# Batched softmax and memory denominators in the second attention, with PSUM evacuations given to ScalarE

## The reference

```python
def step(carry, seg):
    M, z = carry
    qs, ks_, vs = seg
    sq = jax.nn.elu(qs) + 1.0
    sk = jax.nn.elu(ks_) + 1.0
    num_q = einsum('bhld,bhde->bhle', sq, M)
    den_q = einsum('bhld,bhd->bhl', sq, z)[..., None] + EPS
    a_mem = num_q / den_q
    num_k = einsum('bhld,bhde->bhle', sk, M)
    den_k = einsum('bhld,bhd->bhl', sk, z)[..., None] + EPS
    v_delta = vs - num_k / den_k
    M_new = M + einsum('bhld,bhle->bhde', sk, v_delta)
    z_new = z + sk.sum(axis=2)
    scores = einsum('bhld,bhmd->bhlm', qs, ks_) * inv_sqrt_dk
    scores = where(causal_mask, scores, finfo.min)
    a_dot = einsum('bhlm,bhme->bhle', softmax(scores), vs)
    a = gate * a_mem + (1.0 - gate) * a_dot
    return ((M_new, z_new), a)
```

## Time and profile before

| What | Value |
|---|---|
| median of 2 timed runs | 10,834.65 us (10,738.39 and 10,930.91) |
| profiled execution, its own time | 10,657.9 us |
| span in that execution, slowest core | 10,656.3 us (all cores 10,609.8 to 10,656.3) |
| busy on the slowest core | TensorE 5,201.5 us (49%), VectorE 3,776.5 (35%), ScalarE 2,896.8 (27%) |
| weight loads of TensorE | 2,420.8 us, beside its matmuls |
| mean granted TensorE clock | 0.70 of 2.4 GHz |

### The profile page before, as it was taken

How to read it: one execution, slowest core, us unless ns; L and a number is a source line. 1 busy time by engine, 2 the same in 40 slices (tenths; PEclk the granted TensorE clock), 3 DMA queues, 4 the chain that set the end, 5 groups by cost and what they waited for, 6 DMA issues and landing times.

```text
span 10656.3 us, 90473 instructions; the slowest of 8 cores (10609.8 to 10656.3 us)
## 1 busy us (share of the span) xinstructions
PE 5201.5 (49%) x25664; PEld 2420.8 (23%) x25664; DVE 3776.5 (35%) x11485; ACT 2896.8 (27%) x5090; POOL 8.6 (0%) x13
## 2 busy tenths in 40 slices
PE   3856333325585633332558563333254856333326
PEld 1322111112232311111223221111122322111113
DVE  1123344453112334445311233444531123344443
ACT  4222222222322222222132232222213223222221
POOL 0000000000000000000000000000000000000000
PEclk9877555557797855555779775555577977555558
DMA  2001000000101100001010110000101001000010
GB/s 67 12 32 38 10 1 1 16 32 32 63 16 32 34 14 1 1 16 32 32 63 16 32 36 12 1 1 16 32 33 62 16 32 40 9 1 1 16 32 32
DMA packets 69509, 257.50 MB, mean 24 GB/s; under 512 B 7584, under 2 KB 7584, under 8 KB 69024
## 3 DMA queue, kind: packets, MB, share of 16 engines
q1 hardware_dynamic: 50592, 184.60, 5.2%
q10 hardware_dynamic: 18432, 67.12, 2.0%
HBM read 218.14 MB, written 33.55 MB: 24 GB/s over the span
## 4 chain that ended last, share of the span: by engine, by line
PE 39%; DVE 26%; ACT 12%; issue 12%; DMA 9%; DVEq 2%; ACTq 0%; SPq 0%
PE pb L169 35%; PE pb L182 4%; DVE a L682 3%; ACT xn_tm L414 2%; DMA x_tm<-x 2%; ACT ebuf L889 2%; DVE xn_tm L1027 2%; DVE a L981 2%; DVEq L1158 2%; DVE ptbuf L937 2%; ACT warena L303 2%; DVE xn_tm L1049 1%; DVE a L910 1%; DVE a L675 1%; ACT ebuf L897 1%
## 5 line engine op out<-in xcount | busy, mean ns | idle before, releaser
L169 PE MATMUL pb<-a,warena 128*128 128x512 bf16 x6144 | 1446.3, 397 | 343.6 <-DVE a L682 156.8
L169 PE MATMUL pb<-xn_fm,warena 128*128 128x512 bf16 x5120 | 1170.7, 393 | 77.8 <-ACT xn_fm L448 51.3
L169 PE MATMUL pb<-xn_tm,ptbuf 128*128 128x512 bf16 (+1 forms) x3328 | 693.3, 351 | 611.8 <-DVE ptbuf L937 542.0
L169 PEld LDWEIGHTS pb<-a,warena 128*128 128x128 bf16 x6144 | 614.7, 102 | 1153.7 <-issue 540.8
L349 ACT ACTIVATE junkb<-x_tm 128x1024 bf16<-128x1024 f32 x256 | 270.4, 1056 | 2007.3 <-DVE x_tm L580 679.5
L182 PE MATMUL pb<-identb,xn_tm 128*128 128x128 bf16 x2304 | 243.9, 282 | 1084.8 <-ACT xn_tm L414 848.7
L169 PE MATMUL pb<-ebuf,warena 128*128 128x512 bf16 x2048 | 530.5, 425 | 416.6 <-DVE a L746 389.8
L1036 PE MATMUL pb<-xn_tm 128*128 128x128 bf16 x512 | 135.3, 264 | 1133.4 <-DVE xn_tm L1027 1133.4
L169 PEld LDWEIGHTS pb<-xn_fm,warena 128*128 128x128 bf16 x5120 | 510.9, 100 | 724.8 <-issue 192.0
L182 PE MATMUL pb<-identb,ebuf 128*128 128x128 bf16 x2304 | 288.1, 262 | 690.0 <-DVE ebuf L903 690.0
L169 PEld LDWEIGHTS pb<-xn_tm,ptbuf 128*128 128x128 bf16 x3328 | 299.5, 106 | 967.8 <-issue 776.1
(11 more groups left out here) (102 smaller groups left out, 6055.9 us busy)
## 6 DMA issues: line engine op xcount, KB each, us to landing
out<-x_tm SPq DMA_DIRECT2D x64, 512.0 KB, 2.7
warena<-wkfT ACTq DMA_DIRECT2D x48, 512.0 KB, 3.3
warena<-wrT SPq DMA_DIRECT2D x48, 512.0 KB, 3.4
warena<-wvfT SPq DMA_DIRECT2D x48, 512.0 KB, 3.3
x_tm<-x SPq DMA_DIRECT2D x48, 512.0 KB, 3.3
warena<-wqaT SPq DMA_DIRECT2D x24, 512.0 KB, 4.4
warena<-wkaT ACTq DMA_DIRECT2D x24, 512.0 KB, 3.3
warena<-wqb SPq DMA_DIRECT2D x24, 512.0 KB, 4.4
```

Of the source, the lines that this page charges most:

```text
L169: return e.matmul(out, lhsT, rhs, start=st, stop=sp)
```

## The change

The computation stays the same; five things differ, all in `emit_attn_b` (a column `bepscol` that holds epsilon is set up at the start):

1. In `passA` the copy of the transposed blocks to `ptbuf` is made by ScalarE instead of VectorE.
2. The row sums of the four blocks go to separate columns of `dsc`. One addition, one reciprocal and one scaling of 128x4 per head follow after the fourth block, where each block had its own three. A 128x1 memset of the first column is new.
3. The A·V products of the four blocks go side by side into bank 4. After the fourth block ScalarE evacuates them with four scaled activations of 128x128.
4. In `passB` eight matmuls with one column each give the denominators of all four blocks, for Q and K, in bank 5. ScalarE evacuates them with epsilon as bias, VectorE makes one reciprocal of 128x8 and one gate product of 128x4. The numerator matmuls have 128 columns instead of 132. The six small operations per block are gone. The value delta has the opposite sign, and the memory update subtracts it.
5. The gated memory answer is added into `adbuf` in place, and one addition of 128x4x128 per head puts it into `x_tm`, where each block had its own.

```diff
 passA(h), per block lc:
-                        pte = evac(2, "vector", lambda e, lc=lc: e.tensor_copy(
+                        pte = evac(2, "scalar", lambda e, lc=lc: e.copy(
                                        ptbuf[:, 0:lc + 1, :],
                                        pbb[2][:, 0:128 * (lc + 1)]),
                                    waits=[ptm] + buf_war.get("ptbuf", []))
-                        adm = mm_group(ab_, mms, waits=[pte, vt_last])
-                        ads = evac(ab_, "vector", lambda e, ab_=ab_, lc=lc: e.tensor_scalar(
-                                       out=adbuf[:, 128 * lc:128 * lc + 128],
-                                       in0=pb[ab_].ap()[:, 0:128],
-                                       scalar1=dsc[:, 4:5], scalar2=None, op0=ALU.mult),
-                                   waits=[adm, sdm] + buf_war.get(("ad", h % 2, lc), []))
+                        for j in range(lc + 1):
+                            def fad(e, j=j, lc=lc, h=h, st=st, sp=sp):
+                                return e.matmul(
+                                    pb[4].ap()[:, 128 * lc:128 * lc + 128],
+                                    ptbuf[:, j, :],
+                                    xn_tm[:, 4 + j, 128 * h:128 * h + 128],
+                                    start=st, stop=sp)
 passA(h), after the four blocks:
+                    zsum = dv(lambda e: e.tensor_tensor(
+                        out=dsc[:, 36:40], in0=dsc[:, 36:40],
+                        in1=dsc[:, 40:44], op=ALU.add), waits=[z2m, e1, z0m])
+                    rzb = dv(lambda e: e.reciprocal(dsc[:, 40:44], dsc[:, 36:40]), waits=[zsum])
+                    sdb = dv(lambda e, omgcol=omgcol: e.tensor_scalar(
+                        out=dsc[:, 44:48], in0=dsc[:, 40:44],
+                        scalar1=omgcol, scalar2=None, op0=ALU.mult), waits=[rzb])
+                    for lc in range(4):
+                        ads = evac(4, "scalar", lambda e, lc=lc: e.activation(
+                                       out=adbuf[:, 128 * lc:128 * lc + 128],
+                                       in_=pb[4].ap()[:, 128 * lc:128 * lc + 128],
+                                       func=AF.Identity, scale=dsc[:, 44 + lc:45 + lc]),
+                                   waits=[adm_l[3], sdb])
 passB(h), ahead of the four blocks:
+                    denm = mm_group(5, [(sqkv[:, u, h, 128 * lc:128 * lc + 128],
+                                         Maug[:, h, 128:129],
+                                         pb[5].ap()[:, 2 * lc + u:2 * lc + u + 1])
+                                        for lc in range(4) for u in range(2)],
+                                    waits=maug_ready + [el_m[1]])
+                    dev = evac(5, "scalar", lambda e: e.activation(
+                        out=dsc[:, 16:24], in_=pb[5].ap()[:, 0:8],
+                        func=AF.Identity, bias=bepscol[:, 0:1]), waits=[denm])
+                    rbm = dv(lambda e: e.reciprocal(dsc[:, 24:32], dsc[:, 16:24]), waits=[dev])
+                    gqb = dv(lambda e, gcol=gcol: e.tensor_scalar(
+                        out=dsc[:, 32:36], in0=rcp[:, :, 0:1],
+                        scalar1=gcol, scalar2=None, op0=ALU.mult), waits=[rbm])
 passB(h), per block lc:
-                               Maug[:, h, :], pb[3].ap()[:, 0:132]),
+                               Maug[:, h, 0:128], pb[3].ap()[:, 0:128]),
...
-                        d1 = dv(lambda e: e.tensor_scalar(
-                            out=dsc[:, 5:6], in0=pb[3].ap()[:, 128:129],
-                            scalar1=B_EPS, scalar2=None, op0=ALU.add), waits=[nm])
...
                         vdm = dv(lambda e, h=h, lc=lc: e.scalar_tensor_tensor(
-                            out=vd_b, in0=pb[3].ap()[:, 132:260],
-                            scalar=dsc[:, 10:11],
+                            out=vd_b, in0=pb[3].ap()[:, 128:256],
+                            scalar=rcp[:, lc, 1:2],
                             in1=xn_tm[:, 4 + lc, 128 * h:128 * h + 128],
-                            op0=ALU.mult, op1=ALU.add),
-                            waits=[rkn] + buf_war.get("vd", []))
+                            op0=ALU.mult, op1=ALU.subtract),
+                            waits=[nm, gqb] + buf_war.get("vd", []))
+                        c1_last = dv(lambda e, h=h, lc=lc: e.scalar_tensor_tensor(
+                            out=adbuf[:, 128 * lc:128 * lc + 128],
+                            in0=pb[3].ap()[:, 0:128],
+                            scalar=dsc[:, 32 + lc:33 + lc],
+                            in1=adbuf[:, 128 * lc:128 * lc + 128],
+                            op0=ALU.mult, op1=ALU.add), waits=[vdm])
 passB(h), after the four blocks:
+                    c2 = dv(lambda e, G=G, h=h, adbuf=adbuf: e.tensor_tensor(
+                        out=x_tm[:, 4 * G:4 * G + 4, 128 * h:128 * h + 128],
+                        in0=adbuf.rearrange("p (l c) -> p l c", l=4),
+                        in1=x_tm[:, 4 * G:4 * G + 4, 128 * h:128 * h + 128],
+                        op=ALU.add), waits=[c1_last])
```

More of the change, by code:

```diff
@@ L874, in passA @@
                     adbuf = adbuf_a if h % 2 == 0 else adbuf_b
+                    z0m = dv(lambda e: e.memset(dsc[:, 36:37], 0.0),
+                             waits=buf_war.get("zb1", []),
+                             tag=f"{tag}z0_{G}_{h}")
+                    e1 = z2m = None
+                    adm_l, pte_l = [], []
                     for lc in range(4):
@@ L941, in passA @@
                                    tag=f"{tag}pte{G}_{h}_{lc}")
+                        pte_l.append(pte)
                         buf_war[("E", par)] = [ptm]
[L943 to L949 removed]
@@ new lines, in passA @@
+                        adm_l.append(adm)
+                        buf_war["ptbuf"] = [adm]
+                    zsum = dv(lambda e: e.tensor_tensor(
+                        out=dsc[:, 36:40], in0=dsc[:, 36:40],
+                        in1=dsc[:, 40:44], op=ALU.add),
+                        waits=[z2m, e1, z0m], tag=f"{tag}zs_{G}_{h}")
+                    rzb = dv(lambda e: e.reciprocal(dsc[:, 40:44],
+                                                    dsc[:, 36:40]),
+                             waits=[zsum], tag=f"{tag}rz_{G}_{h}")
@@ new lines, in passA @@
+                    buf_war["zb1"] = [rzb]
+                    sdb = dv(lambda e, omgcol=omgcol: e.tensor_scalar(
+                        out=dsc[:, 44:48], in0=dsc[:, 40:44],
+                        scalar1=omgcol, scalar2=None, op0=ALU.mult),
+                        waits=[rzb] + buf_war.get("zb_sd", []),
+                        tag=f"{tag}sd_{G}_{h}")
+                    ads = None
+                    for lc in range(4):
+                        ads = evac(4, "scalar",
+                                   lambda e, lc=lc: e.activation(
+                                       out=adbuf[:, 128 * lc:128 * lc + 128],
+                                       in_=pb[4].ap()[:, 128 * lc:128 * lc + 128],
+                                       func=AF.Identity,
+                                       scale=dsc[:, 44 + lc:45 + lc]),
+                                   waits=[adm_l[3], sdb] +
+                                         buf_war.get(("ad", h % 2, lc), []),
```

123 lines of the change are left out of this document (46 added, 77 removed).

## The result

| | before | after |
|---|---|---|
| median of the timed runs | 10,746.56 us (10 runs, 10,620.18 to 10,930.91) | 10,199.43 us (11 runs, 10,123.16 to 10,399.37) |
| profiled execution, its own time | 10,657.9 us | 10,240.26 us |
| fastest execution | 10,620.18 us | 10,123.16 us |

The ratio after to before is **0.9487, 95% interval 0.9434 to 0.9540**: faster by 5.1%. The forecast ratio was 0.963. In some executions one or both groups of four cores had a lower granted clock, which adds up to 4% whatever the kernel, so the ratios with an interval leave these out, and elsewhere I read single heads or the fastest execution.

What follows compares the result with a forecast made beforehand. A latency chain with handovers, not one full engine, bounds the kernel. Terms of -399, -2, -82, +40 and +50 sum to -393 us: 10,657.9 becomes 10,265, or 10,435 on the median; range 10,250 to 10,600, widened to 10,220 to 10,670.

Steps and rivals of the forecast that it cites:

- A: passA: copy on ScalarE and softmax sums normalised once per head, from mask to A·V; gain 1.12 us per middle head.
- B: Four scaled evacuations stand ahead of the elu operations in ScalarE's queue; loss 2.96 us per middle head.
- C: Entry into passB, from its transposes to the first wide operation, with grouped denominators; gain 0.91 us per head.
- D: passB's loop of four blocks: six small operations go, spacing 3.03 to 1.45 us; gain 4.74 us per head.
- E: One 512-wide addition replaces four narrow ones and delays the next mask; loss 0.25 us per middle head.
- first passA of a segment: passA's gain there is eaten by the evacuations ahead of the next exponential; -0.1 us, 16 times.
- last passB of a segment: No passA before it and its elu ran ahead anyway; -5.15 us, 16 times, -82 in all.
- segment's end: Four row statistics wait for the one addition; loss 3.2 us in 12 segments, 0.4 in 4 before the FFN, +40.
- weight conversions: In a sequence's last segment, conversions on ScalarE lose their cover beside passB; loss 12.6 us, 4 times, +50.
- denominators: Rival: passB's one-column matmuls are not pipelined, 0.37 us each; 10,709 us; chance 0.09, shared with larger ScalarE waits.
- the clock: Rival: TensorE gets its full clock in the head loop, some 2 us less a head; 10,175 us; chance 0.05.
- function table loads: Rival: ScalarE reloads its function table between copies and exponentials, ten loads a head; 12,100 us, slower; chance 0.02.

Runs made afterwards that it cites:

- x9: The kernel before with one column per block for the first partial row sum, so most L889 wait for TensorE alone; a head 31.57 us instead of 31.70.
- x1: The changed kernel with passA as it was before, passB as changed; a head 25.91 us, fastest execution 0.940 of before.
- x2: The kernel before with the new passA only, passB as before; a head 32.77 us, fastest execution 1.011 of before.
- x10: The changed kernel with VectorE's sum over the keys moved behind the first block of passB's loop; a head 26.63 us, fastest execution 0.950 of before.

## Why the prediction was right in its direction and short in size

| term | forecast | measured | times | difference, us |
|---|---|---|---|---|
| A, passA's copies and sums | -1.12 | -1.78 | 112 | -74 |
| B, evacuations ahead of elu | +2.96 | +2.94 | 112 | -2 |
| C, entry into passB | -0.91 | -1.08 | 112 | -19 |
| D, loop of four | -4.74 | -4.84 | 112 | -11 |
| E, addition and next mask | +0.25 | +0.04 | 112 | -24 |
| first passA of a segment | -0.1 | -0.8 | 16 | -11 |
| last passB of a segment | -5.15 | -5.6 | 16 | -7 |
| segment's end | +3.2 | +5.5 | 12 | +28 |
| weight conversions | +12.6 | +10.2 | 4 | -10 |

A is measured from the first mask to the last A·V group, B from there to passB's transposes, the conversions as what a sequence's last segment takes beyond the others (12.9 us, before 2.7).

Summed with the measured terms the third layer becomes some 525 us shorter (4,744 to 4,220, core 1 before and core 4 after), the rest of the program 19 longer. The whole of these cores goes from 10,609.8 to 10,104.3, -505, a ratio of 0.952; the forecast was -393.

**The step that failed is A**, -74 of the -130 us by which the terms missed, in two sentences of it. "Score, exponentials and mask between stay" was wrong: from A·V to the next mask the three stretches shrank by 0.19 in all, of which the second wait explains most (x9: 0.12). The diff showed the wait going: "[waits sPE,sDV]" became "[waits sPE]". I had read that row and priced nothing. And "Back to TensorE I put 0.20" was too much: it is 0.14, as for VectorE (1299.54 + 0.27 to 1299.95). With copies and handovers slightly shorter than in my sum, mask to A·V sums to 5.83 instead of 6.17. The last 0.12 lies in the base: the means of before are 7.41, where I read 7.29 from one head without its stalls.

**B and D** held in mechanism and size, which x1 and x2 confirm by splitting them. Four evacuations took 1.14 from the first start to the last end. What the sum needs is the time to the next operation's start, and that was 1.02 (1283.74 to 1284.76), forecast 1.12; the three handovers took back 0.07 of it. By the figures of the page "ScalarE: Activation LUTs" of the Trainium skill, section "What ACT_TABLE_LOAD costs", that step was an estimated 1.2. The trace has 0.36 to 0.38 for one evacuation where they give 0.386, and 1.02 for the step. The spacing in D is 1.43 in the mean, where 1.45 was forecast.

**C** came out near for the wrong reason. I priced a one-column matmul like a transpose, 0.105. The group of eight takes 0.40, and one of them 0.17 in the mean:

```profile
L170 PE MATMUL pb<-a 128*128 128x1 bf16 x1024 | 50.7, 171 | 0.0
```

So they start some 0.03 apart, (0.40 - 0.17) / 7, which is below my lower bound of 0.05; in the single records the first gap is 0.07 and the other six are 0.027. The twelfth matmul ended 0.78 after the first transpose began, not 1.43, and the evacuation was done 0.48 before the reciprocal started. "VectorE is past its copy and its sum over the keys by then" failed: that sum (L1010) set the end (x10). The page "TensorE: Matmul & The Clock Gate" of the Trainium skill, section "Wait — 56ns, not 53.3ns?", puts the floor at 25 ns, and the trace agrees within 2 ns. The 0.64 that I worked out from this rule was there on TensorE (1.43 to 0.78), and the wait for the sum hid it.

**E**: I let the mask wait for the whole addition and memset. It starts 0.07 before the addition ends, and the memset runs beside it. In the first passA of a segment I had let the evacuations eat A's gain; most of it stayed (0.8).

**The segment's end** has the right mechanism, "now all four wait for the one addition", and too low a price: the statistics follow each other at 1.24, not at 1.06, since each is followed by a read of its accumulator (0.19 in the timeline), so TensorE starts 3.7 later instead of 3.2. The rest, some 1.8 us, comes after that, from TensorE's clock (the segment's end, above), and the prediction had no term for it.

**The rivals fell as argued:** denominators 0.03 apart and not 0.37; the clock at 0.50 in the head window; function table loads 17 before and after, 8 of them at the line that was L704 (now L706), none in a head.

**The base moved too.** The forecast stood on a median of two runs, 10,834.65; with ten it is 10,746.56, 0.8% lower. The forecast ratio on that gives 10,350 and the range 10,137 to 10,583, which would have held the result. Term A made the forecast too small; the base moved the range off. Two ratios of the prediction are rounded wrongly: -39 of 10,657.9 is 0.996 and -529 is 0.950; the times beside them fit these.

## What to carry to other kernels

In a chain of short handovers, an operation moved to a less busy engine still costs its length if it lands ahead of that engine's next link in the chain. Look for what stands behind it in the queue, and place it behind the latency-critical operations: here that alone was worth 2 us of 27 per head. Price waits that go or come as well as work, and split a change that gains and loses into halves: one half here was faster than the whole.
